# A gated attention and feed-forward block on one core: all five engines' hand-out of work in another order, with other PSUM banks

## The reference

```python
x = L0_attn_x                                  # (8, 512, 256), float32
xn = _layernorm(x, axis=-1)
s = attention(xn)                              # 16 heads of 16, RoPE on q and k, causal softmax, then @ wo + bo
g = _silu(ffn(xn))                             # (silu(xn @ wg.T) * (xn @ wu.T)) @ wd.T, hidden 768, int weights / 127
return x + s * g
```

## Time and profile before

| | us |
|---|---|
| median of the runs shown | 553.73 |
| lowest and highest of the 3 | 550.44, 556.63 |
| the profiled execution, its own time | 555.2 |
| span of its profile | 553.7 |

### The profile page before, as it was taken

One profiled execution on the slowest core, in us unless ns is written; L12 is line 12 of the kernel. 1 busy time (PEld: TensorE's weight loads), 2 busy tenths in 40 slices (PEclk: granted clock), 3 DMA queues, 4 the chain that ended last, 5 costly groups with the idle time before them and its releaser, 6 DMA issues.

```text
span 553.7 us, 13804 instructions
## 1 busy us (share of the span) xinstructions
PE 480.0 (87%) x5397; PEld 367.7 (66%) x5397; DVE 425.1 (77%) x667; ACT 330.0 (60%) x683; POOL 332.1 (60%) x439
## 2 busy tenths in 40 slices
...
PEclk9989799997999999999999999999989989977988
...
GB/s 290 110 178 167 83 53 135 114 213 128 105 75 212 197 160 181 158 130 148 170 140 95 223 85 88 160 176 216 136 93 134 164 174 155 158 151 64 3 78 38
DMA packets 59667, 76.65 MB, mean 138 GB/s; under 512 B 15056, under 2 KB 30928, under 8 KB 59600
## 3 DMA queue, kind: packets, MB, share of 16 engines
...
q10 hardware_dynamic: 1088, 1.05, 0.6%
...
## 4 chain that ended last, share of the span: by engine, by line
PE 38%; DVE 25%; DMA 13%; ACT 8%; issue 7%; SPq 6%; POOL 2%; DVEq 0%; ACTq 0%; POOLq 0%
PE ps_w L618 22%; DVE row_max L982 9%; PE ps_w L749 5%; DMA sum_rows<-o_t 5%; PE ps_w L647 4%; ACT probs L863 4%; PE ps_w L663 4%; DMA at_lo<-inv_rows 4%; DVE h_lo L434 3%; DVE hid L1028 2%; DVE hid L1023 2%; DVE attn L991 2%; PE ps_w L650 2%; DVE high_low L972 1%; SPq L549 1%
## 5 line engine op out<-in xcount | busy, mean ns | idle before, releaser
L982 DVE TENSOR_REDUCE row_max<-ps_w 128x2 f32<-128x1024 f32 (+3 forms) x256 | 199.7, 815 | 42.0 <-PE ps_w L650 41.6
L863 ACT ACTIVATE probs<-ps_w 128x512 f32<-128x512 f32 (+1 forms) x384 | 181.0, 535 | 78.1 <-PE ps_w L663 65.2
L1094 POOL TENSOR_SCALAR_AFFINE_SELECT probs<-probs 128x256 f32<-128x256 f32 x256 | 109.4, 449 | 123.1 <-ACT probs L863 122.9
L647 PE MATMUL ps_w<-k_st,q_st 48*128 48x512 f32 (+3 forms) x512 | 80.8, 355 | 19.5 <-DVE row_max L982 6.5
L663 PE MATMUL ps_w<-q_st,k_st 49*128 49x512 f32 (+3 forms) x512 | 78.8, 353 | 16.0 <-DMA q_st<-minus_max 5.8
L618 PE MATMUL ps_w<-xt_hi,wgu_hi 64*128 64x512 f32 x384 | 84.9, 430 | 3.0 <-DVE wgu_lo L961 1.3
L618 PE MATMUL ps_w<-xt_lo,wgu_hi 64*128 64x512 f32 x384 | 80.4, 407 | 0.0
L749 PE MATMUL ps_w<-probs,vals 128*32 128x512 f32 (+3 forms) x1024 | 79.1, 450 | 0.7 <-POOL probs L1094 0.4
L647 PEld LDWEIGHTS ps_w<-k_st,q_st 48*128 48x128 f32 x512 | 49.1, 195 | 39.8 <-issue 11.8
L663 PEld LDWEIGHTS ps_w<-q_st,k_st 49*128 49x128 f32 x512 | 47.2, 193 | 35.0 <-ACT probs L863 8.7
L749 PEld LDWEIGHTS ps_w<-probs,vals 128*32 128x32 f32 x1024 | 29.1, 112 | 41.0 <-issue 29.7
...
## 6 DMA issues: line engine op xcount, KB each, us to landing
...
```

Of the source, the lines that this page charges most:

```text
L647: pe.matmul(dst[h][:, col:col + (t + 1) * P], q_st[64 * h:64 * h + STACK, pair, t * P:(t + 1) * P], k_st[64 * h:64 * h + STACK, pair, 0:(t ...
L863: nc.scalar.activation(probs[:, (pair % 2) * SLOTS + slot, col:col + WIDTH[c]], w_of(kind, b, 3 * pair + c // 2, c % 2)[:, 0:WIDTH[c]], AC ...
L982: last = nc.vector.tensor_reduce(of_pair, both_of(kind, b, i)[:, :, col:col + (t + 1) * P], AX.X, ALU.max)
L1094: nc.gpsimd.affine_select(out=v, in_=v, compare_op=ALU.is_ge, fill=0.0, base=0, pattern=[[0, 2], [1, P]], channel_multiplier=-1).then_inc( ...
```

## The change

Every step stays, with the same instructions, sizes and semaphores; the counts that a wait asks for follow the lists. What changes is the place of the steps in the five lists and the bank numbers in PE's. SP's list is a line shorter, so every later line of the file has a number lower by one (L543 of before is L542 after). Of the diff a line or two of two lists stand here; the rest reads alike:

```diff
@@ ORDER, "sp" @@
-        WS2.1 WS3.1 RL0.0 MD2.0 RD0.1 RD1.1 NA1.0 MD3.0 WS0.2 NC0.0 WS1.2 NB1.0 ND0.0 NA2.0 MD0.1 NC1.0 RD2.1 ND1.0 NB2.0 NA3.0 NB3.0 NC2.0
+        WS2.1 WS3.1 NB0.0 MD2.0 RD0.1 WS0.2 NC0.0 RD1.1 MD3.0 NA1.0 WS1.2 NB1.0 RD2.1 NA2.0 MD0.1 ND0.0 NB2.0 NC1.0 NA3.0 NB3.0 NC2.0 ND1.0
...
@@ ORDER, "pe" @@
-        A16.0@01 B8.0@45 QK0.2@67 B9.0@23 A17.0@01 QK1.2 A18.0@01 B10.0@23 DN0.1@45 B11.0@67 A19.0@01 A20.0@23 DN1.1 MT2.0@01 PV1.0@2
+        B7.0@01 QK0.2@23 A17.0@67 B8.0@45 QK1.2 B9.0@01 DN0.1@45 MT2.0@67 A18.0@01 A19.0@23 B10.0@67 DN1.1 A20.0@67 QK2.2@01 A21.0@23
...
```

PE's list, from the turn of the maxima of group 2 in batch 0 (MT2.0) to the second A step of batch 1, before and after:

```diff
-MT2.0@01 PV1.0@2 A21.0@01 QK2.2@34 A22.0@56 QK3.2 A23.0@01 B12.0@27 G0.2@56 A0.1@01 B13.0@23 U0.2 B14.0@47 MT3.0@01 A1.1@01
+MT2.0@67 A18.0@01 A19.0@23 B10.0@67 DN1.1 A20.0@67 QK2.2@01 A21.0@23 B11.0@67 QK3.2 B12.0@46 A22.0@23 PV1.0@7 B13.0@01 A23.0@23 A0.1@45 G0.2@67 A1.1@23
```

and at the two other places where the prediction speaks of PE's list (MT3.1 to B18.1, and MT3.6 to B18.6):

```diff
-MT3.1@01 B16.1@34 QK2.3@56 A0.2@01 B17.1@34 QK3.3 A1.2@34 B18.1@01
+MT3.1@01 QK2.3@23 B17.1@01 A0.2@67 QK3.3 A1.2@01 PV2.1@6 A2.2@01 B18.1@27
...
-MT3.6@67 A0.7@23 B17.6@04 A1.7@67 PV2.6@0 B18.6@12
+MT3.6@45 U5.7 A1.7@45 B17.6@67 PV2.6@0 A2.7@34 B18.6@15
```

More of the change, by code:

```diff
@@ L111 @@
-        B10.1@24 MT2.1@56 A18.1@56 OP0.0@01 A19.1@23 B11.1@47 OP1.0 XT0.3@45 XT1.3@67 PV1.1@2 B12.1@34 QK0.3@56 B13.1@07 A20.1@12 B14.1@34
-        QK1.3 A21.1@01 DN0.2@27 B15.1@01 A22.1@34 A23.1@56 DN1.2 MT3.1@01 B16.1@34 QK2.3@56 A0.2@01 B17.1@34 QK3.3 A1.2@34 B18.1@01 PV2.1@2
-        A2.2@34 B19.1@01 A3.2@56 B20.1@27 A4.2@34 B21.1@01 A5.2@56 G0.3@27 A6.2@01 B22.1@34 A7.2@56 U0.3 G1.3@01 B23.1@34 MT0.2@56 U1.3
-        A8.2@56 A9.2@23 PV3.1@4 A10.2@56 A11.2@23 B0.2@07 V0.3@14 B1.2@56 V1.3 MT1.2@23 B2.2@05 G2.3@67 A12.2@23 B3.2@01 U2.3 A13.2@45
@@ new lines @@
+        A16.4@67 B10.4@34 OP0.3@05 A17.4@12 A18.4@67 XT0.6@34 MT2.4@12 OP1.3 B11.4@67 XT1.6@12 PV1.4@3 A19.4@45 B12.4@67 QK0.6@01 B13.4@23
+        A20.4@45 B14.4@67 QK1.6 B15.4@23 A21.4@45 DN0.5@67 A22.4@01 A23.4@23 B16.4@45 DN1.5 B17.4@01 MT3.4@23 QK2.6@45 A0.5@23 QK3.6 A1.5@01
+        PV2.4@2 A2.5@01 B18.4@34 A3.5@56 B19.4@27 A4.5@01 A5.5@34 B20.4@56 G0.6@27 A6.5@01 B21.4@56 A7.5@34 U0.6 G1.6@01 B22.4@56 A8.5@34
+        U1.6 V0.6@25 MT0.5@34 B23.4@67 V1.6 A9.5@34 A10.5@67 PV3.4@0 G2.6@34 A11.5@67 B0.5@01 U2.6 A12.5@56 G3.6@07 B1.5@12 B2.5@56 U3.6
@@ new lines @@
+        B3.5@13 A13.5@56 G4.6@24 MT1.5@01 U4.6 A14.5@01 B4.5@35 G5.6@67 U5.6 A15.5@01 B5.5@35 PV0.5@2 B6.5@34 A16.5@56 XT0.7@01 XT1.7@23
+        B7.5@47 A17.5@56 B8.5@01 A18.5@23 B9.5@47 B10.5@56 QK0.7@01 A19.5@23 MT2.5@45 QK1.7 A20.5@67 B11.5@45 PV1.5@2 A21.5@01 B12.5@67
+        A22.5@45 OP0.4@23 B13.5@01 B14.5@67 OP1.4 A23.5@01 DN0.6@45 MT3.5@67 A0.6@01 A1.6@23 B15.5@67 DN1.6 A2.6@01 QK2.7@23 A3.6@01
+        B16.5@67 QK3.7 B17.5@46 A4.6@01 PV2.5@7 A5.6@01 B18.5@23 A6.6@45 B19.5@67 A7.6@01 G0.7@23 MT0.6@45 B20.5@67 A8.6@45 A9.6@01 B21.5@67
```

225 lines of the change are left out of this document (110 added, 115 removed).

## The result

The changed kernel takes 530.5 us (four executions, 527.6 to 533.4) where the kernel before takes 553.6 (550.4 to 556.6): a ratio of 0.958, with a 95% interval of 0.951 to 0.966. A later series of six executions gave 531.2 and 0.958 [0.951, 0.964].

What follows compares the result with a forecast made beforehand. PE was taken to bound the kernel, busy 480.0 of 553.7 us, with only its gaps and half clock recoverable. Terms summed to -8.3 us: 555.2 to 546.9, adjusted to 546.0; range 539 to 556.

Steps and rivals of the forecast that it cites:

- B18.1: PE's 1.38 us wait for maxima in batch 1 goes, since product PV2.1 now comes in ahead: -1.4 us.
- tighter places: Steps that the new order brings nearer to what they wait for, at unnamed places: +2.5 us, between 0 and 6.5.
- The end of batch 6: DVE's waits for softmax sums at RC2.6 go and RC3.6 comes sooner: -2.0 us; less half clock there: -1.0.
- The turn: From batch 0 to 1, PE's waits at B12.0 (maxima) and A0.1 (k) nearly go: -3.1 us, between -3.6 and -1.5.
- The clock's part: Half clock behind the turn from batch 0 to 1, 122.5 to 132.7 us, mostly goes: -3.0 us, between -4.5 and 0.
- The start: One more split of k on DVE ahead of the feed-forward's first product: +0.3 us; sign: that product between 38.5 and 41.
- B18.6: PE's 1.27 us wait for maxima in batch 6 about halves, as U5.7 comes in and A0.7 goes out: -0.6 us.
- Half of the 1.5 us of the profiled execution given back: Whole kernel: the profiled execution was 1.5 us above the median, so 546.9 was lowered to a forecast of 546.0.
- That the clock doesn't come back: Rival for the whole kernel: waits go, but clock falls hang on short idles at bank changes; 549.5 to 551 us, chance 0.18.
- That the waits only move: Rival: PE's gaps move to the steps behind, since DVE has the same work in any order; 553.5 us, chance 0.12.
- That DVE's waits for sums stand in the way: Rival: reciprocals nearer their products stop DVE, then PE; 561 us, DVE's waits for sums above 25 us, chance 0.14.

Runs made afterwards that it cites:

- the table: Not one run: profiled executions having before's or after's order in each of four stretches of PE's work, compared at equal work; after's order is 24.6 us shorter in sum.
- The kernel up to the turn: After's lists on all engines up to 126 us (start and turn from batch 0 to 1), before's order and banks behind; 546.9 us, 0.988 of before.
- before with after's reads: The kernel before with only the steps of values and sums (SyncE, DVE, ACT, all batches) put where after has them; 564.9 us, 1.016 of before.

## Why the prediction was wrong in size

Against the table's 24.6 us the sum has -8.3. Start and turn are -5.8 in it and measured -4.2. Batches 1 to 5 are +1.1 (-1.4 for B18.1, and the +2.5 for tighter places, wherever they are, counted here) and measured -10.6: this step failed most, since nothing but one wait was set against the tighter places. The end of batch 6 and what follows is -3.6 and measured -9.8: this term was sized too small.

**The turn, -3.1 of waits and -3.0 of clock.** The mechanism stands: with RL0.0 directly ahead MD2.0 lands 5.5 to 8.8 us after its issue (nine profiles, median 6.6), without it after 2.7 to 5.5 (eleven, median 3.6; 3.6 and 3.3 in the two that change SyncE's list alone), and after has neither wait. The size was read from an execution that lost more there than others. The kernel up to the turn gained 6.7 us, of which the start has 3.6, which leaves some 3 for the turn, with an interval that takes in 0 and the 6.1; at equal work it is 2.7. The clock's part, -3.0, rests on a fall that three of seven kernels with this turn have. The start I had at +0.3; the first product of the feed-forward came at 40.55 us, inside the 38.5 to 41 that I had asked for, and that the start gains all the same shows that the place was the wrong one to look at.

**The end of batch 6, -2.0, -1.0 of clock and -0.6 for B18.6.** RC2.6's wait went as worked out and RC3.6 has its sums 5.6 us after PV3.6 instead of 11.7. (What stands newly ahead of RC2.6 are four maxima and one low part, 3.01 us and some 0.9, not three and one in 3 us; it changes nothing.) But the stretch from the end of batch 5 on gives 9.8 us, not 3.6: idle places before and behind the two reciprocals went as well, and the half clock there fell from 26.3 to 13.4 us, which is 6.4 us of PE's time, where I had allowed 1.0 and at most 3.3. I had looked at the half clock at 487.7 and 498 us and at none of that at 450, 529, 542 and 553.

**B18.1, -1.4 and B18.6, -0.6.** B18.1 waits no more. B18.6 waits 1.13 us, so 0.1 was gained and not 0.6.

**Tighter places, +2.5.** They are there: A0.2 waits 2.20 us (under 0.5 in before), B0.1 1.05, B0.3 1.08. But I set nothing except B18.1 against them. The two middle stretches, batches 1 to 5, where I had +2.5 and -1.4, gave 5.3 us each: that is the missing term, 10.6 us. No single place shows it. One wait that shrinks much is ACT's for the products (13.7 us in 8 places, 2.8 in 3 after), and I had read the waits of PE, DVE and SP only. That reading alone would have given a wrong cause, too: taking those waits away by themselves moved them to DVE.

**Half of the 1.5 us of the profiled execution given back.** Right in sign and beside the point: executions of before differ by 17 us of span, most of it along with how much half clock they catch.

**The rivals.** That the clock doesn't come back (549.5 to 551) is refuted for after, whose half clock is 27 us against 56 in the profiled executions and with whose clock 8.5 to 10.5 of the 23 us go. (Its upper figure is slightly off: two waits of 1.3 us more make 552, not 551.) The rule of the Trainium skill behind it ("TensorE: Matmul & The Clock Gate", second failure mode) isn't contradicted all the same: filling five long holes of before left the half clock about where it was (49 and 51 us), so the long holes are not its only cause; whether the short idles are the other, no run here shows. That the waits only move (553.5) is what happens in the two kernels that move a few steps of one engine (553.7 and 552.3), and what does not happen when all five change together. That DVE's waits for sums stand in the way (561, to be seen above 25 us) is wrong for after, whose waits are 15.6 us. With SyncE's list alone DVE waits 19.6 us for sums and 8.3 for their inverses, and the time is 593.8, so there the mechanism is at least part of it; before with after's reads is slower too (564.9), but with 8.5 us of waits for sums, so not by this mechanism, and by which stays open.

**What stays open.** Which steps make the two middle stretches shorter no run shows below whole stretches, so the cause of the missing 10.6 us is known by its place only. Nor does any run part the bank numbers from the order of PE's list. Why the clock falls in one execution and not in the next with the same list isn't explained by any run.
